# Gate and up products of a mixture of experts in split parts, z heads 4 to 7 moved behind the output products, one activation table for Tanh and Silu

## The chip, the cores and the metric

The kernel runs on one core of a Trainium2 chip, as one launch. The metric is the device time of that launch in microseconds (us), median of several runs. The core has five engines with queues of their own: PE (TensorE, matrix products; PEld is its weight load), DVE (VectorE), ACT (ScalarE), POOL (GpSimd) and SP (SyncE, which issues all DMAs here). They meet only at semaphores.

## The reference

x is 128 tokens of 256 values; ctx is 12544 rows of 256. Three blocks follow one another, each on a layer-normalised x and added to it.

```
x = x + cross_attention(layernorm(x), ctx)            # softmax over 12544 keys
x = x + delta_and_moe(layernorm(x))                   # block 2, below
x = x + ffn(layernorm(x))                             # 8 experts, top 2, W1 256x1024, W2 1024x256

# block 2, input n = layernorm(x)
q, k, v, z = split(rms(n) @ W_qkvz)                   # z: 8 heads of 128
q, k, v = silu(causal_conv4(q, k, v)); g, beta from rms(n) @ W_ba
core = gated_delta_rule(q, k, v, g, beta)             # 8 heads, a recurrence over 128 tokens
core = core * rsqrt(mean(core^2) + eps) * gate_norm * silu(z)
h = n + core @ W_out
y = rms(h)
top two of softmax(y @ W_router), their weights normalised to sum 1 -> route
moe = sum_e route[e] * (silu(y @ W_gate[e]) * (y @ W_up[e])) @ W_down[e]   # 8 experts of 128
out = h + moe
```

The mixture of block 2 takes 256 inputs to 8 experts of 128 (1024 columns) twice, once for gate and once for up.

## The kernel before

All of it stands in one function, `perceiver`, with one block of code per engine; the order of the code is the order of each engine's queue, and `then_inc` / `wait_ge` on named semaphores tie the queues together. There is no scheduler.

Up to about 98 us the cross attention streams ctx in 14 groups. Then come the projections of block 2, and from 119.6 us the delta rule, whose triangular inverse is built in six levels (`for lv in range(1, LEVELS)`). In each level and each half b of the heads PE multiplies pairs (L676), transposes (L457), and multiplies again (L689); DVE masks the first product (`Tm`, L1284) and adds the second to the state (L1300); ACT copies the transposes (`copy_xt`, L967). The state after the add is what the next level's first product waits for. The z heads are projected in between by `project_z(h)`, two products of 128x128x128 each (L462): head 2 in level 2 and heads 3, 5, 7 in the gaps of levels 3, 4, 5 (`Z_GAPS`), heads 4 and 6 at the ends of levels 3 and 4 (`Z_ENDS`).

Behind the levels: Z (L700), the output products o = Z Bv (L707, half b into bank 5 + b), the mean square of o per head (ACT squares L1005, L1008; DVE sums L1315, L1317), its root on ACT (L1012) and reciprocal on DVE (L1323), the product of o and silu(z) (L1319), the scaling of heads by that factor shared by DVE (L1327) and ACT (L1016), `core_transposes` on PE, a scaled copy `coreT` on ACT (L1020) and `project_out` (L718). `keep_warm(n)` (L453) is n products on a constant tile, whose result nobody reads.

Then h (L1334), its transposes, the router product, and `gate_up(b, o, w)`: four times two products that multiply 128 inputs into 512 columns, in plain fp32 (L462). A plain fp32 product shows as two MATMUL records in the trace, a product of fp32r parts as one. Beside it DVE finds the top two experts and their weights (`gates`, L1346 to L1356, then L1361); ACT computes the tangent of the difference (L1029) and Silu of the gate (L1033); DVE multiplies gate, route and up (`prod`, L1368); PE transposes `prod` (`products`), ACT copies it (L1037), and `downs` (L745) multiplies by W_down. Last comes the feed-forward block with 8 large experts, from about 174.5 us, in which weights arrive by DMA into four slots. Slots 2 and 3 lie in `late_slots`, and their first loads wait for the last attention product.

Already in this kernel large products of the attention and of the last block use a split: a matrix a is rounded to fp32r (hi) by a copy, lo = a - hi is rounded too, and three products hi*hi, lo*hi and hi*lo are added in PSUM.

## Time and profile before

| | us |
|---|---|
| median of 3 runs | 232.85 (232.74 to 232.89) |
| the profiled execution's own time | 232.53 |
| its span, first to last instruction | 230.6 |
| PE busy | 221.5 (96%) |
| DVE busy | 143.3 (62%) |
| ACT busy | 143.9 (62%) |
| POOL busy | 122.2 (53%) |

The span leaves out 1.9 us around the first and the last instruction. PE's ends are modelled, so a busy PE need not be limited by its own work. A chain of waits, followed back from the last instruction, tells which work ended last; 74% of it lies on PE. DMA is busy until 121 us (ctx, the weights of block 2, four experts) and again from 178 to 207 us (experts 4 to 7), and idle between.

### The profile page before, as it was taken

Reading aid. Unit: us, or ns where it says so; the run is one execution under the profiler, and the core shown is the slowest. Engines: PE = TensorE matmul, PEld = TensorE weight load, DVE = VectorE, ACT = ScalarE, POOL = GpSimd, SP = SyncE. Lnnn points to the kernel's source line nnn. Section 1 sums busy time; section 2 is a strip of 40 time slices with the busy share of each in tenths; the row PEclk is TensorE's granted clock in tenths of the full one; section 3 lists DMA queues with packets and bytes.
Section 4 is the critical chain, followed back from the end, with each engine's and each line's share of the span. In section 5 each row is a group of like instructions: output and inputs, shape, how many; then the busy total and the mean of one; then the engine's idle time right before and its main releaser. Section 6 shows DMA issues by size and latency. Waiting matters only on the chain.

```text
span 230.6 us, 4195 instructions
## 1 busy us (share of the span) xinstructions
PE 221.5 (96%) x1559; PEld 194.0 (84%) x1559; DVE 143.3 (62%) x339; ACT 143.9 (62%) x264; POOL 122.2 (53%) x80
## 2 busy tenths in 40 slices
PE   8999999999999999889979999989999999999994
PEld 7757878888888888879969999864789999999993
DVE  2346666666666667356995776444334769887783
ACT  5257697777777775348776557545317848677570
POOL 1139878888888897732799910000000544555550
PEclk9999999999999999999999999999999999999999
DMA  6999999999999706999960000000000686960000
GB/s 200 393 430 415 416 420 418 415 418 416 414 419 417 293 3 229 424 423 421 418 283 0 4 0 3 0 0 0 1 3 0 203 345 239 411 259 7 0 0 23
DMA packets 8532, 52.94 MB, mean 230 GB/s; under 512 B 953, under 2 KB 1218, under 8 KB 6466
## 3 DMA queue, kind: packets, MB, share of 16 engines
q1 hardware_dynamic: 8514, 52.69, 56.9%
q8 instruction: 12, 0.20, 0.4%
q14 instruction: 6, 0.05, 0.1%
HBM read 52.56 MB, written 0.13 MB: 228 GB/s over the span
## 4 chain that ended last, share of the span: by engine, by line
PE 74%; DVE 9%; DMA 7%; ACT 4%; POOL 3%; issue 2%; ACTq 0%; DVEq 0%; POOLq 0%
PE psum L462 25%; PE psum L542 11%; PE psum L794 8%; DMA late_sb<-in_ctx_T 7%; PE psum L457 6%; PE psum L518 5%; PE psum L453 3%; PE psum L689 3%; PE psum L676 3%; POOL ctx_lo L375 2%; PE psum L718 2%; PE psum L745 1%; PE psum L560 1%; DVE work L1233 1%; DVE ring L1271 1%
## 5 line engine op out<-in xcount | busy, mean ns | idle before, releaser
L445 POOL TENSOR_TENSOR h_lo<-ring,h_hi 128x512 fp32r<-128x512 f32 x16 | 24.8, 1548 | 67.0 <-ACT h_hi L1061 61.0
L375 POOL TENSOR_TENSOR ctx_lo<-ring,ctx_hi 128x1792 fp32r<-128x1792 f32 x13 | 52.6, 4045 | 14.1 <-ACT ctx_hi L860 14.1
L462 PE MATMUL psum<-late_sb,work 128*128 128x448 f32 x68 | 27.8, 541 | 0.0
L462 PE MATMUL psum<-xT,late_sb 128*128 128x128 f32 x224 | 26.2, 276 | 0.1
L867 ACT ACTIVATE probsT_hi<-psum 128x512 fp32r<-128x512 f32 (+1 forms) x28 | 13.7, 540 | 19.3 <-PE psum L457 18.0
L462 PEld LDWEIGHTS psum<-xT,late_sb 128*128 128x128 f32 x224 | 25.5, 192 | 0.3 <-DVE xT L1377 0.3
L860 ACT ACTIVATE ctx_hi<-ring 128x1792 fp32r<-128x1792 f32 x13 | 22.1, 1701 | 3.4 <-DMA ring<-in_ctx 3.4
L1121 DVE TENSOR_REDUCE smalls<-psum 128x1 f32<-128x896 f32 x14 | 15.3, 1092 | 14.3 <-PE psum L518 9.1
L1145 DVE TENSOR_TENSOR probsT_lo<-psum,probsT_hi 128x512 fp32r<-128x512 f32 (+1 forms) x28 | 16.2, 619 | 7.3 <-ACT probsT_hi L867 7.1
L462 PEld LDWEIGHTS psum<-late_sb,work 128*128 128x128 f32 x68 | 11.9, 190 | 8.1 <-issue 7.8
L457 PE MATMUL psum<-early_sb,work 128*128 128x128 f32 x122 | 17.1, 274 | 0.3 <-ACT work L1016 0.3
L542 PE MATMUL psum<-ctx_hi,probsT_hi 128*128 128x256 f32 x91 | 15.5, 286 | 0.5 <-POOL ctx_lo L375 0.5
L453 PE MATMUL psum<-warm 128*128 128x128 f32 x100 | 14.3, 300 | 1.0 <-POOL smalls L362 1.0
L542 PE MATMUL psum<-ctx_hi,probsT_lo 128*128 128x256 f32 x91 | 15.2, 284 | 0.0
L542 PE MATMUL psum<-ctx_lo,probsT_hi 128*128 128x256 f32 x91 | 15.1, 282 | 0.0
L457 PEld LDWEIGHTS psum<-early_sb,work 128*128 128x128 f32 x122 | 13.9, 143 | 1.3 <-ACT work L850 0.7
L462 PE MATMUL psum<-xT,late_slots 128*128 128x128 f32 x128 | 14.9, 275 | 0.0
L542 PEld LDWEIGHTS psum<-ctx_hi,probsT_hi 128*128 128x128 f32 x91 | 13.5, 189 | 1.4 <-DVE O L1132 0.7
L462 PEld LDWEIGHTS psum<-xT,late_slots 128*128 128x128 f32 x128 | 14.6, 192 | 0.0
L453 PEld LDWEIGHTS psum<-warm 128*128 128x128 f32 x100 | 13.6, 214 | 1.1 <-POOL smalls L362 1.0
L1407 DVE TENSOR_TENSOR w_lo<-late_sb,w_hi 128x1024 fp32r<-128x1024 f32 x8 | 13.6, 1701 | 1.2 <-ACT w_hi L1066 0.8
L850 ACT ACTIVATE work<-psum,smalls 128x896 f32<-128x896 f32 x14 | 14.2, 1011 | 0.1
(262 smaller groups left out, 493.5 us busy)
## 6 DMA issues: line engine op xcount, KB each, us to landing
late_sb<-in_ctx_T SPq DMA_DIRECT2D x14, 896.0 KB, 14.2
ring<-in_ctx SPq DMA_DIRECT2D x14, 896.0 KB, 13.2
late_sb<-in_late SPq DMA_DIRECT2D x10, 825.0 KB, 11.2
late_sb<-in_experts SPq DMA_DIRECT2D x8, 1024.0 KB, 9.9
late_slots<-in_experts SPq DMA_DIRECT2D x8, 1024.0 KB, 11.9
early_sb<-in_early SPq DMA_DIRECT2D x1, 512.0 KB, 3.6
early_sb<-in_early SPq DMA_DIRECT2D x1, 465.0 KB, 17.8
work<-in_levels SPq DMA_DIRECT2D x1, 416.0 KB, 19.1
```

The source lines that it names most:

```text
L375: nc.gpsimd.tensor_tensor(ctxNv[1][:, r % 2], ring[:, r], ctxNv[0][:, r % 2], ALU.subtract).then_inc(s["ctx_lo"], 1)
L445: nc.gpsimd.tensor_tensor(hT[1][:, e % 2, at, :], h32[:, at, :], hT[0][:, e % 2, at, :], ALU.subtract).then_inc(s["h_lo_done"], 1)
L453: nc.tensor.matmul(bank[7][:, 0:P], warm[:, :], warm[:, :], start=True, stop=True)
L457: last = nc.tensor.transpose(o, i, ident)
L462: last = nc.tensor.matmul(o, lhs(c), rhs(c), start=(c == 0), stop=(c == n - 1))
L542: last = nc.tensor.matmul(bank[6 + r % 2][:, 0:D], probsT[a][:, t, :], ctxNv[b][:, r % 2, t, :], start=(i == 0), stop=(i == len(terms) - 1))
L794: last = nc.tensor.matmul(bank[1 + e % 2][:, 0:D], hT[a][:, e % 2, n, :], w2[b][:, e % 2, n, :], start=(t == 0), stop=(t == len(terms) - 1))
L850: nc.scalar.activation(probs[:, :].rearrange("p (z k) -> p z k", z=2), psum[:, 2 * b:2 * b + 2, 0:HALF], ACT.Exp, bias=s_("nb", b, b + 1), ...
L860: nc.scalar.activation(ctxNv[0][:, r % 2], ring[:, r], ACT.Copy).then_inc(s["ctx_hi"], 1)
L867: nc.scalar.activation(probsT[0][:, 4 * q:4 * q + tiles, :], bank[4 + q][:, 0:tiles * P].rearrange("p (t q) -> p t q", q=T), ACT.Copy).the ...
L1121: V.tensor_reduce(s_("mx"), psum[:, 2 * b:2 * b + 2, 0:HALF], mybir.AxisListType.XY, ALU.max).then_inc(s["mx_done"], 1)
L1145: V.tensor_tensor(probsT[1][:, 4 * q:4 * q + tiles, :], bank[4 + q][:, 0:tiles * P].rearrange("p (t q) -> p t q", q=T), probsT[0][:, 4 * q ...
```

## The change

Five edits come together.

1. Gate and up weights are split into hi (ACT, `gate_up_hi(i)`) and lo (POOL, `gate_up_lo(i)`), four pieces of 2 x 512 columns each, in the order of `GATE_UP`; the normalised h, transposed, is split as well (`x2_parts`). `gate_up(i)` on PE is six fp32r products in place of two plain ones. The parts lie where slots 2 and 3 are, so the first loads of these slots now wait for the last of the four `gate_up`.
2. The z heads 4 to 7 leave levels 3, 4 and 5 and follow the output products, ahead of `keep_warm(4)`, which was `keep_warm(10)`. `silu_z(1)` on ACT moves from level 5 to behind the squares of o. In its place in level 5 stands `gate_up_hi(0)`, and `gate_up_hi(1)` stands where the preload of the Sqrt table was.
3. The factor of the mean square is one power of -0.5 on POOL for each half, in place of a root on ACT and a reciprocal on DVE. DVE scales seven heads and ACT one (head 3). The first head's part of `project_out` goes ahead of the second `core_transposes`.
4. Silu's table is loaded ahead of Tanh, by a Silu on a spare value right after the last Sqrt; the separate table load before Silu is gone.
5. `gates` takes fewer dependent steps: route = (e1 + e2) + th (e1 - e2), with the weight already in e1 and e2. The add `xh` moves from ahead of the route to behind it.

The names in the following rows are tiles: `late_sb` holds the weights of block 2, `ring` and `work` are reused buffers, `xT` the transposed input, `warm` the constant tile.

PE, level 4 of the delta rule, from its second half's transposes to the first product of level 5, before:

```order
L457 MATMUL psum<-early_sb,work 128x128 x2
L689 MATMUL psum<-ring 128x128 [waits xt_done,t_done]
L689 MATMUL psum<-ring 128x128
L462 MATMUL psum<-late_sb,xT 128x128 x2
L689 MATMUL psum<-ring 128x128 [waits xt_done,t_done]
L689 MATMUL psum<-ring 128x128
L462 MATMUL psum<-late_sb,xT 128x128 x2
L676 MATMUL psum<-ring,work 128x128 [waits x_done,xc_done,al_high]
```

and now:

```order
L476 MATMUL psum<-early_sb,work 128x128 x2
L708 MATMUL psum<-ring 128x128 [waits xt_done,t_done]
L708 MATMUL psum<-ring 128x128
L708 MATMUL psum<-ring 128x128 [waits xt_done,t_done]
L708 MATMUL psum<-ring 128x128
L695 MATMUL psum<-ring,work 128x128 [waits x_done,xc_done,al_high]
```

Both z heads (L462, two products each) have left this level; nothing stands between its last product and the wait for the state.

PE, from the second half of the output products to `project_out`, before:

```order
L707 MATMUL psum<-ring,work 128x128 [waits zs_done,bv_done,zb_done]
L707 MATMUL psum<-ring,work 128x128 x3
L453 MATMUL psum<-warm 128x128 x10
L457 MATMUL psum<-early_sb,work 128x128 [waits core_act,core_dve]
L457 MATMUL psum<-early_sb,work 128x128 x3
L453 MATMUL psum<-warm 128x128 x4
L457 MATMUL psum<-early_sb,work 128x128 [waits core_act,core_dve]
L457 MATMUL psum<-early_sb,work 128x128 x3
L718 MATMUL psum<-late_sb,ring 128x256 [waits coreT_done]
```

and now:

```order
L724 MATMUL psum<-ring,work 128x128 [waits zs_done,bv_done,zb_done]
L724 MATMUL psum<-ring,work 128x128 x3
L481 MATMUL psum<-late_sb,xT 128x128 x8
L472 MATMUL psum<-warm 128x128 x4
L476 MATMUL psum<-early_sb,work 128x128 [waits core_act,core_dve]
L476 MATMUL psum<-early_sb,work 128x128 x3
L472 MATMUL psum<-warm 128x128 x4
L738 MATMUL psum<-late_sb,ring 128x256 [waits coreT_done]
L476 MATMUL psum<-early_sb,work 128x128 [waits core_dve]
L476 MATMUL psum<-early_sb,work 128x128 x3
```

Eight z products stand where six of the warm ones were, and one product of `project_out` lies between the two sets of transposes.

DVE, from the logits' copy to the first product with the route, before:

```order
L1359 COPY smalls<-psum 128x8 [waits lg_mm,dve_chain]
L1346 MAX smalls<-smalls 128x8 [waits dve_chain]
L1347 MAX_INDEX topi<-smalls 128x8 [waits dve_chain]
L1348 TENSOR_SCALAR smalls<-smalls 128x1 [waits dve_chain]
L1349 CAST smalls<-topi 128x8
L1350 TENSOR_SCALAR smalls<-early_sb,smalls 128x8 [waits dve_chain]
L1351 TENSOR_SCALAR smalls<-early_sb,smalls 128x8 [waits dve_chain]
L1353 TENSOR_SCALAR smalls<-smalls 128x1 [waits tanh_done,dve_chain]
L1354 TENSOR_SCALAR smalls<-smalls 128x1 [waits dve_chain]
L1355 TENSOR_SCALAR smalls<-smalls 128x8 [waits dve_chain]
L1356 SCALAR_TENSOR_TENSOR smalls<-smalls 128x8 [waits dve_chain]
L1361 TENSOR_SCALAR smalls<-smalls 128x8 [waits dve_chain]
```

and now:

```order
L1417 COPY smalls<-psum 128x8 [waits lg_mm,dve_chain]
L1401 MAX smalls<-smalls 128x8 [waits dve_chain]
L1402 MAX_INDEX topi<-smalls 128x8 [waits dve_chain]
L1403 TENSOR_SCALAR smalls<-smalls 128x1 [waits dve_chain]
L1404 CAST smalls<-topi 128x8
L1405 TENSOR_SCALAR smalls<-early_sb,smalls 128x8 [waits dve_chain]
L1406 TENSOR_SCALAR smalls<-early_sb,smalls 128x8
L1409 TENSOR_TENSOR smalls<-smalls 128x8 [waits dve_chain]
L1410 TENSOR_TENSOR smalls<-smalls 128x8
L1414 SCALAR_TENSOR_TENSOR smalls<-smalls 128x8 [waits tanh_done,dve_chain]
L1419 TENSOR_TENSOR xb<-x,hh 128x256 [waits dve_chain]
```

Four of the steps behind the indices are gone and two are new, the wait for the tangent sits at the last one, and the 256-column add (L1419) now lies between the route and its first use.

The core of the diff:

```diff
-Z_GAPS = {2: 2, 3: 3, 4: 5, 5: 7}
-Z_ENDS = {3: 4, 4: 6}
...
-                    sp.wait_ge(s["pv_done"], NG)
+                    sp.wait_ge(s["gu_mm"], 4)
...
+            def gate_up_lo(i):
+                w, b = GATE_UP[i]
+                pool.wait_ge(s["gu_hi"], i + 1)
+                nc.gpsimd.tensor_tensor(gate_up_parts[1][:, w, :, b, :], gate_up_32[:, w, :, b, :], gate_up_parts[0][:, w, :, b, :],
+                                        ALU.subtract).then_inc(s["gu_lo"], 1)
+
+            gate_up_lo(0)
+            for b in range(2):
+                pool.wait_ge(s["ms_done"], b + 1)
+                nc.gpsimd.tensor_tensor(s_("f", 4 * b, 4 * b + 4), s_("ms", 4 * b, 4 * b + 4), s_("marks", 7, 8).to_broadcast([P, 4]), ALU.pow)\
+                    .then_inc(s["f_done"], 1)
+            for i in range(1, 4):
+                gate_up_lo(i)
...
-                if lv in Z_ENDS:
-                    project_z(Z_ENDS[lv])
...
-            keep_warm(10)
+            for h in range(4, HV):
+                project_z(h)
+            keep_warm(4)
             def core_transposes(b):
                 pe.wait_ge(s["core_dve"], b + 1)
-                pe.wait_ge(s["core_act"], b + 1)
+                if b == 0:
+                    pe.wait_ge(s["core_act"], 1)
...
+            project_out(range(0, 1))
             core_transposes(1)
-            project_out(range(0, 4))
+            project_out(range(1, 4))
...
-            def gate_up(b, o, w):
-                wide(bank[o + b][:, :], lambda c: half(xT, c), lambda c: w[:, c, 512 * b:512 * (b + 1)]).then_inc(s["gu_mm"], 1)
+            wide(bank[7][:, 0:E], lambda c: half(xT, c), lambda c: w_router[:, c, :]).then_inc(s["lg_mm"], 1)
+            pe.wait_ge(s["x2_hi"], 2)
+
+            def gate_up(i):
+                w, b = GATE_UP[i]
+                pe.wait_ge(s["gu_hi"], i + 1)
+                terms = [(u, v, c) for u, v in ((0, 0), (0, 1), (1, 0)) for c in range(DC)]
+                for t, (u, v, c) in enumerate(terms):
+                    if t == DC:
+                        pe.wait_ge(s["gu_lo"], i + 1)
+                    if t == 2 * DC:
+                        pe.wait_ge(s["x2_lo"], 2)
+                    last = nc.tensor.matmul(bank[3 + 2 * w + b][:, :], half(x2_parts[u], c), gate_up_parts[v][:, w, c, b, :],
+                                            start=(t == 0), stop=(t == len(terms) - 1))
+                last.then_inc(s["gu_mm"], 1)
...
+            gate_up(0)
+            gate_up(1)
+            gate_up(2)
             products(0)
-            gate_up(1, 5, w_up)
+            gate_up(3)
...
+            def gate_up_hi(i):
+                w, b = GATE_UP[i]
+                if i == 0:
+                    act.wait_ge(s["late2_in"], 16 * (LATE_PARTS - FIRST_PARTS))
+                nc.scalar.activation(gate_up_parts[0][:, w, :, b, :], gate_up_32[:, w, :, b, :], ACT.Copy).then_inc(s["gu_hi"], 1)
...
-            silu_z(1)
+            gate_up_hi(0)
             copy_xt(6)
             keep_columns(6)
-            nc.scalar.activation(s_("spare", 0, 1), s_("eps", 3, 4), ACT.Sqrt).then_inc(s["act_chain"], 1)
-            chain[0] += 1
+            gate_up_hi(1)
...
-                act.wait_ge(s["ms_done"], b + 1)
-                nc.scalar.activation(s_("f", 4 * b, 4 * b + 4), s_("ms", 4 * b, 4 * b + 4), ACT.Sqrt).then_inc(s["f_sd"], 1)
-                act.wait_ge(s["f_done"], b + 1)
-                for k in (2, 3):
-                    h = 4 * b + k
-                    last = nc.scalar.activation(core[:, h, :], core[:, h, :], ACT.Copy, scale=s_("f", h, h + 1))
-                last.then_inc(s["core_act"], 1)
+            silu_z(1)
+            act.wait_ge(s["zo_done"], 1)
+            act.wait_ge(s["f_done"], 1)
+            nc.scalar.activation(core[:, 3, :], core[:, 3, :], ACT.Copy, scale=s_("f", 3, 4)).then_inc(s["core_act"], 1)
             for b in range(2):
                 act.wait_ge(s["core_T"], b + 1)
                 nc.scalar.activation(coreT[:, 4 * b:4 * b + 4, :], bank[3 + b][:, :].rearrange("p (h t) -> p h t", h=4), ACT.Copy,
                                      scale=early_at("gate_norm")).then_inc(s["coreT_done"], 1)
+                if b == 0:
+                    gate_up_hi(2)
+            nc.scalar.activation(s_("spare", 0, 1), s_("eps", 3, 4), ACT.Sqrt).then_inc(s["act_chain"], 1)
+            chain[0] += 1
+            gate_up_hi(3)
...
+            nc.scalar.activation(half(x2_parts[0], 1), bank[2][:, 0:P], ACT.Copy, scale=s_("w2p", 1, 2)).then_inc(s["x2_hi"], 1)
             link(nc.scalar.activation(scratch[:, :], hh[:, :], ACT.Square, accum_out=s_("sd", 0, 1)))
             nc.scalar.activation(s_("sd", 1, 2), s_("sd", 0, 1), ACT.Sqrt, scale=1.0 / D, bias=s_("eps", 2, 3)).then_inc(s["hsd_done"], 1)
+            nc.scalar.activation(s_("spare", 0, 1), s_("eps", 3, 4), ACT.Silu).then_inc(s["act_chain"], 1)
+            chain[0] += 1
...
+            mean_squares(0)
+            gate_output(0)
+            mean_squares(1)
+            normalize(0, range(0, 3))
+            gate_output(1)
+            normalize(1, range(4, HV))
...
+            V.tensor_scalar(half(x2_parts[0], 0), bank[1][:, 0:P], s_("w2p", 0, 1), None, ALU.mult).then_inc(s["x2_hi"], 1)
+            dve.wait_ge(s["x2_hi"], 2)
+            for c in range(DC):
+                V.scalar_tensor_tensor(half(x2_parts[1], c), bank[1 + c][:, 0:P], s_("w2p", c, c + 1), half(x2_parts[0], c),
+                                       ALU.mult, ALU.subtract).then_inc(s["x2_lo"], 1)
...
+                V.tensor_scalar(s_("e1"), early_at("iota"), s_("idf", 0, 1), weight, ALU.is_equal, ALU.mult).then_inc(s["dve_chain"], 1)
+                V.tensor_scalar(s_("e2"), early_at("iota"), s_("idf", 1, 2), weight, ALU.is_equal, ALU.mult).then_inc(s["dve_chain"], 1)
+                chain[0] += 2
+                dve.wait_ge(s["dve_chain"], chain[0])
+                V.tensor_tensor(s_("lg"), s_("e1"), s_("e2"), ALU.subtract).then_inc(s["dve_chain"], 1)
+                V.tensor_tensor(s_("top"), s_("e1"), s_("e2"), ALU.add).then_inc(s["dve_chain"], 1)
+                chain[0] += 2
+                dve.wait_ge(s["dve_chain"], chain[0])
                 dve.wait_ge(s["tanh_done"], turn)
-                link(V.tensor_scalar(s_("w", 0, 1), s_("th"), 0.5, 0.5, ALU.mult, ALU.add))
-                link(V.tensor_scalar(s_("w", 1, 2), s_("th"), -0.5, 0.5, ALU.mult, ALU.add))
-                link(V.tensor_scalar(s_("e1"), s_("e1"), s_("w", 0, 1), None, ALU.mult))
-                return V.scalar_tensor_tensor(out, s_("e2"), s_("w", 1, 2), s_("e1"), ALU.mult, ALU.add)
+                return V.scalar_tensor_tensor(out, s_("lg"), s_("th"), s_("top"), ALU.mult, ALU.add)
...
-            link(V.tensor_copy(s_("lg"), bank[1][:, D:D + E]))
-            link(gates(s_("route"), 1, s_("rs", 0, 1)))
-            link(V.tensor_scalar(s_("route"), s_("route"), s_("rs", 0, 1), None, ALU.mult))
+            link(V.tensor_copy(s_("lg"), bank[7][:, 0:E]))
+            link(gates(s_("route"), 1, s_("rs", 0, 1), s_("w", 0, 1)))
+            link(V.tensor_tensor(xh[:, :], x1[:, :], hh[:, :], ALU.add))
```

## Rows read from the trace of the kernel before

**Rows 1.** The page: granted TensorE clock in 40 slices of the span, in tenths.

```profile
PEclk9999999999999999999999999999999999999999
```

**Rows 2.** Chain of waits, 125 us to the end: start us, us, what.

```profile
132.88 0.45 PE psum L462 x4
...
141.46 1.06 PE psum L707 x8
...
145.91 0.63 PE psum L457 x4
...
148.00 3.59 PE psum L718 x16
...
163.95 2.01 PE psum L745 x8
...
192.80 2.87 PE psum L794 x24
```

**Rows 3.** Timeline, levels 1 and 4 to 6: start us, us, engine line operation, [idle before <-releaser].

```profile
119.64 0.68 PE L676 MATMUL psum<-ring 128*128 128x128 f32 x4 [0.62 <-DVE ring L1271]
...
129.86 0.65 PE L676 MATMUL psum<-work 128*128 128x128 f32 x4
...
131.30 0.68 PE L689 MATMUL psum<-ring 128*128 128x128 f32 x4
...
132.02 0.72 DVE L1300 TENSOR_TENSOR ring<-work,psum 128x256 f32<-128x256 f32 x1
...
133.16 0.61 PE L676 MATMUL psum<-ring,work 128*128 128x128 f32 x4
...
136.41 0.64 PE L676 MATMUL psum<-ring,work 128*128 128x128 f32 x4
...
139.50 1.95 PE L700 MATMUL psum<-ring,work 128*128 128x128 f32 x16
```

**Rows 4.** Timeline and POOL's instructions by form, the output stage.

```profile
143.12 2.31 PEld L453 LDWEIGHTS psum<-warm 128*128 128x128 f32 x20
...
143.99 0.16 DVE L1317 SCALAR_TENSOR_TENSOR smalls<-smalls 128x4 f32<-128x4 f32 x1
...
145.07 0.69 ACT L1016 ACTIVATE work<-work,smalls 128x128 f32<-128x128 f32 x2 [0.40 <-DVE smalls L1323]
145.07 0.48 DVE L1327 TENSOR_SCALAR work<-work,smalls 128x128 f32<-128x128 f32 x2
...
L438 POOL TENSOR_TENSOR smalls<-smalls 128x4 f32<-128x4 f32 x1 | 1.1, 1061 | 0.0
```

**Rows 5.** Timeline, from the router's product to the first product with the route.

```profile
153.13 5.86 PE L462 MATMUL psum<-late_sb,xT 128*128 128x8 f32 x16
...
154.49 0.17 DVE L1359 COPY smalls<-psum 128x8 f32<-128x8 f32 x1
...
155.69 1.28 ACT L1033 ACT_TABLE_LOAD   x1
...
156.99 0.69 ACT L1033 ACTIVATE ring<-psum,smalls 128x512 f32<-128x512 f32 x1
156.99 0.23 DVE L1361 TENSOR_SCALAR smalls<-smalls 128x8 f32<-128x8 f32 x1
...
157.78 1.12 DVE L1368 SCALAR_TENSOR_TENSOR ring<-ring,smalls,psum 128x128 f32<-128x128 f32 x4 [0.55 <-ACT ring L1033]
```

**Rows 6.** Chain of waits, an earlier group: six fp32r products of 448 columns.

```profile
37.55 1.32 PE psum L518 x6
```

**Rows 7.** Instructions by form of 128x1024: the copy to hi, the subtraction.

```profile
L1063 ACT ACTIVATE w_hi<-late_sb 128x1024 fp32r<-128x1024 f32 x4 | 4.2, 1042 | 0.0
...
L399 POOL TENSOR_TENSOR ctx_lo<-ring,ctx_hi 128x1024 fp32r<-128x1024 f32 x1 | 2.4, 2381 | 1.4 <-ACT ctx_hi L896 1.4
```

**Rows 8.** Loads into the slots (line L313), and their first reader in slots 2, 3.

```profile
DMA to landing us min/median/max: 4.9/11.7/21.6
...
181.79 3.40 PE L462 MATMUL psum<-xT,late_slots 128*128 128x128 f32 x29
```

More of the change, by code:

```diff
@@ L99, in perceiver @@
             ctxN = parts(overlay, "ctx", 2 * GT * D)
+        with ExitStack() as overlay:
+            GU = parts(overlay, "gate_up", 2 * DC * E * P)
+        assert 4 * DC * E * P <= (SLOTS - W_SLOTS) * EXPERT_N
         late_slots = sb("late_slots", (SLOTS - W_SLOTS) * EXPERT_N)
@@ L136, in perceiver @@
         w_out = late_at("out", c=HV)
-        w_gate = late_at("gate", c=DC)
-        w_up = late_at("up", c=DC)
         w_down = late_at("down", c=E)
+        gate_up_32 = W_sb[:, LATE["gate"][0]:LATE["up"][1]].rearrange("p (w c b n) -> p w c b n", w=2, c=DC, b=2)
+        gate_up_parts = [part[:, :].rearrange("p (w c b n) -> p w c b n", w=2, c=DC, b=2) for part in GU]
+        x2_parts = [part[:, 0:D] for part in (h_hi, h_lo)]
         w_router = late_at("router", c=DC)
@@ L606, in project_z @@
             def project_z(h):
-                last = wide(bank[5 + h // 4][:, h % 4 * P:(h % 4 + 1) * P], lambda c: half(xT, c),
+                last = wide(bank[5 if h < 4 else 2][:, h % 4 * P:(h % 4 + 1) * P], lambda c: half(xT, c),
                             lambda c: w_qkvz[:, c, CONV + P * h:CONV + P * (h + 1)])
@@ L960, in silu_z @@
                 act.wait_ge(s["z_done"], b + 1)
-                nc.scalar.activation(zs[:, 4 * b:4 * b + 4, :], bank[5 + b][:, :].rearrange("p (h t) -> p h t", h=4), ACT.Silu).then_inc(s["zs_done"], 1)
+                nc.scalar.activation(zs[:, 4 * b:4 * b + 4, :], bank[5 if b == 0 else 2][:, :].rearrange("p (h t) -> p h t", h=4), ACT.Silu).then_inc(s["zs_done"], 1)
             def copy_xt(lv):
@@ L1309, in _, with mean_squares @@
             values(1)
-            dve.wait_ge(s["zs_done"], 2)
             dve.wait_ge(s["n2_read"], 1)
-            for b in range(2):
+            def mean_squares(b):
                 dve.wait_ge(s["osq_done"], b + 1)
@@ L1341, in _, with gates @@
             dve.wait_ge(s["x2_done"], 1)
-            link(V.tensor_tensor(xh[:, :], x1[:, :], hh[:, :], ALU.add))
-            def gates(out, turn, scale):
+            link(V.tensor_scalar(s_("w", 0, 1), s_("rs", 0, 1), 0.5, None, ALU.mult))
+            def gates(out, turn, scale, weight):
                 link(V.max(s_("top"), s_("lg")))
@@ L1385, in _ @@
             link(V.tensor_tensor(s_("lg"), bank[0][:, D:D + E], early_at("rb2"), ALU.add))
-            gates(s_("gate"), 2, 1.0).then_inc(s["gate_done"], 1)
+            gates(s_("gate"), 2, 1.0, 0.5).then_inc(s["gate_done"], 1)
             dve.wait_ge(s["gate_done"], 1)
```

54 lines of the change are left out of this document (24 added, 30 removed).

## The prediction

> **What bounds the kernel now.** I read the page first, then the chain of waits, then the timeline of the three stretches that the change touches. The page has PE busy for 96% of the span (table above), at the full clock of 2.4 GHz in every slice [rows 1]; it does not show whether that is work or warm products. The chain of waits does. In the levels of the delta rule PE's products, the z heads among them, follow one another without a gap, and each z head is a link of 0.45 us [rows 2]. From the output products to the first transposes of `core` (141.46 + 1.06 = 142.52 to 145.91) the chain leaves PE for ACT and DVE, and PE only runs warm products [rows 2, 4]. Then PE again: `project_out`, 3.59 us; the router's and three gate and up products, 5.86 us; `downs` [rows 2, 5]. In the last block PE's 24 products of 2.87 us repeat for each expert [rows 2], and nothing of it is touched except that four loads come later. So three terms decide: A, the levels; B, the stage of the output; C, gate and up with the route.
>
> **A, z heads 4 to 7 out of the levels.** Removed are four heads of 0.45 us [rows 2], 1.8 us of PE in levels 3 (one), 4 (two) and 5 (one). How much of it comes back depends on what is late next. I walk through level 4, from 129.86 to 133.16, 3.30 us [rows 3]. Its second products start after 1.44 us, at 131.30; DVE's add of the first half starts 0.72 us behind that, at 132.02, and takes 0.72 [rows 3]; with a hand-over of 0.05 it releases level 5 at 2.93 us. So 0.4 us of the 0.9 come back, and the rest turns into a wait for DVE. In level 3 the head stood at the end, where the add was already done: its whole 0.45 comes back. Level 5 (133.16 to 136.41, 3.25 us) must hold what level 6 holds on PE, which has no head in it and yet takes from 136.41 to 139.50, 3.09 us, since its second pair of products waits for the copy of the transposes [rows 3]. So 0.15 to 0.25 there. Sum 1.1 us (0.45 + 0.4 + 0.2, rounded up by half a hand-over).
>
> The bounds: 1.8 if all comes back. The other end is that levels 3 and 4 can't go below level 6's 3.1 us either, since DVE has about as much to do in each: 0.15 + 0.2 + 0.15 = 0.5 us come back. I take 1.1, since level 6 has the value products on DVE ahead of its adds, which the others lack.
>
> What hides the new work on ACT: `gate_up_hi(0)`, 1.04 us [rows 7], stands where `silu_z(1)` was, in a pause before `copy_xt(6)`; with everything 0.9 us earlier it ends about when these transposes are ready. If it is late, it is by 0.1 to 0.3 us, inside the bounds. `gate_up_hi(1)`, 1.04, replaces a table load of 1.28 [rows 5]. POOL's `gate_up_lo(0)`, 2.38 us [rows 7], ends some 4 us before POOL's first power is wanted.
>
> **B, the output stage.** Call the end of the first output product 0 (142.52 before). Before, the transposes start at 3.39 and h's operand is ready when `project_out` ends, at 148.00 + 3.59 - 142.52 = 9.07 [rows 2]. Now there are two paths. Power path: the sum of squares is ready at 144.15 - 142.52 = 1.63 [rows 4]; POOL's power of 128x4 took 1.06 us [rows 4], with 0.2 for hand-overs, 2.89; three scalings of 0.24 on DVE [rows 4], 3.6. z path: PE's eight z products start where the warm ones did, at 0.6 [rows 4], and end at 2.4, with drain 2.5; `silu_z(1)` 0.69, 3.2; ACT's one scaling 0.35 [rows 4], 3.55, and 0.15 to PE: 3.7. So the transposes start 0.3 us later than before. Behind them the PE queue is shorter: transposes 0.45, four warm products 0.89, transposes 0.45, eight products of `project_out` 3.59, 5.4 us in place of 5.69 (145.91 to 151.60 [rows 2]), because one of the eight now fills the wait for the second `coreT`. That makes 9.1. `gate_up_hi(2)` lies on ACT ahead of the second `coreT` copy, which then ends at 6.95, 0.45 us before PE wants it. Term B: +0.1 us, between -0.2 (the transposes as early as before) and +0.8 (the second `coreT` late by a further copy of 1.04 us [rows 7], less its 0.45 of slack, and 0.2 on the power). Behind that copy ACT's Sqrt table load (1.28) and `gate_up_hi(3)` (1.04) end near 9.3, while DVE adds h and PE transposes it.
>
> **C, gate, up and route.** Times here are those of before. The plain products start behind the router's at about 153.65: they end at 158.99, and there are 12 records of 512/1.2 ns in it [rows 5]. Six fp32r products of 448 columns took 1.32 us [rows 6], and 24 of 256 columns 2.87 [rows 2]; the first scales to 0.25 us for 512 columns, the second, 0.107 + 0.013, gives 0.226. I take 0.226: 1.36 us for each `gate_up` in place of 1.71. The extra copies `x2_hi` (0.3 us on DVE and on ACT) end with the router's product, and `x2_lo` at 154.05, before PE's fifth product. Three `gate_up` end at 157.7.
>
> Who releases the first `prod`? Before, ACT: table load 155.69 to 156.97, Silu to 157.68, then DVE from 157.78 [rows 5]. Now the table load ends at 155.4 and waits for nothing, and Silu of the gate ends at 156.5. DVE becomes the last: its copy of the logits stays at 154.49, since three small operations replace the add that stood there; from there to the route it took 2.73 us [rows 5], and four steps less with two more and fewer hand-overs make 2.1; then the moved add, 0.45. Products from 157.1 to 158.25, transposes at 158.3 in place of 158.95. So PE waits 0.6 us, and 0.35 of the 0.65 gained are spent there. Behind it the last `gate_up` saves 0.35 and its start delay 0.1. From its end the chain is the same as before (products 1.12, transposes, copy, five `downs`). Term C: -0.65 - 0.45 = -1.1 us. Bounds: -0.5 (0.25 us for each product and 0.4 more on DVE's short steps), -1.6 (the route no bound at all).
>
> The ScalarE: Activation LUTs page of the Trainium skill, section What ACT_TABLE_LOAD costs, says that a switch of tables costs a drain of about 1.38 us besides the 1.28 of the load. The rows of this case speak against it: Silu starts at 156.99, 1.30 us after its load's start [rows 5]. By that page Tanh would come at about 156.8, the route 0.6 us later, and the total at 231.3.
>
> **Loads.** The loads of experts 2 and 3 now start when the last `gate_up` is done, at about 158.0 of the new time. Landing took 21.6 us at the longest, with nine loads ahead or beside, and 11.7 at the median [rows 8]. Their first reader comes at 181.8 - 2.1 = 179.7 [rows 8]. So even the longest, 179.6, is just in time. This costs nothing, and the DMA queue had nothing to do between 121 and 178 us.
>
> **Sum.** -1.1 + 0.1 - 1.1 = -2.1 us against the profiled execution's own 232.53, so 230.4. The median of before is 0.3 us above that execution; the forecast for the median is 230.7.
>
> **Rivals.**
> *Levels bound elsewhere.* DVE and the copies set the pace of the levels, as in level 6 [rows 3]; A is 0.5. For it: level 6 is the only level without a head, and it is hardly shorter. Against it: the walk through level 4, whose add could be done 0.4 us sooner. Time 231.3.
> *The gap moves to the output stage.* Power, z path and the second `coreT` are late; B is +0.8. For it: ACT has four jobs more there, each in a fixed place. Against it: 0.45 us of slack at the narrowest. Time 231.4.
> *PE's clock falls* (slower than before). PE now pauses for 0.85 us before the first transposes of `core` and 0.6 before those of `prod`, where warm products or work ran. If the clock granted falls to 1.2 GHz in the first pause, the 5.4 us behind it take twice as long, +5.4, and nothing hides it: 230.7 + 5.4 = 236.1. It decides as soon as 2.1 us of PE work run at half clock. Against it: before, PE paused for 0.62 us at the start of level 1 and the clock stayed full [rows 1].
> *Experts late.* Landing takes over 22 us; each further us costs one, and 2.1 us of it make the kernel as slow as before. With no other traffic I hold this for the least likely.
> *The table's drain*, above: 231.3.
>
> **How the numbers follow.** Forecast 0.58; levels bound elsewhere 0.15; output stage 0.1; drain 0.03; terms that shrink together until 0.2% or less is left (232.4 to 233.3) 0.06; slower, by the clock 0.05 or late experts and the like 0.03. 0.2%, 0.47 us, is about what a measurement of this kernel can tell from no change. All terms at their good ends give -1.8 - 0.2 - 1.6 = -3.6, 229.2; all at their bad ends -0.5 + 0.8 - 0.5 = -0.2, 232.6. Eight times in ten I expect 229.5 to 232.0. Faster 0.86, same 0.06, slower 0.08.
>
> **What would show it.** A: from the first product of level 4 to the first one behind level 6 9.0 us in place of 9.64, and DVE's add named as what ended PE's wait ahead of level 5. B: from the first output product's end to the end of `project_out` 9.1 us, the transposes at 3.7, released by ACT's scaling. C: from the router's product to the end of `downs` 11.7 us in place of 12.8; the transposes of `prod` wait 0.6 us for DVE; 24 products at 0.226 us. I am wrong if level 4 keeps 3.3 us, if PE's clock shows less than full, or if a large product waits for a load in slot 2.

## The result, and the profile after

| us | before | after |
|---|---|---|
| median | 232.87 (12 runs, 232.46 to 233.88) | 235.68 (12 runs, 233.74 to 238.23) |
| ratio, 95% interval | | 1.0093 [1.007, 1.0117] |
| profiled execution, its span | 232.53, 230.6 | 235.96, 234.2 |

The kernel became 0.9% slower by the ratio; the medians are 2.8 us apart. Forecast was 230.7, with 229.5 to 232.0 as the range. The ratio leaves out one run after, the one of 238.23 us, which counts as slow. The page of the kernel after has PE busy for less of a longer span, and one slice of the granted clock below full, where before had none [rows 1]:

```profile
PE 220.9 (94%) x1555; PEld 195.2 (83%) x1555; DVE 147.1 (63%) x341; ACT 145.2 (62%) x264; POOL 133.5 (57%) x86
...
PEclk9999999999999999999999999979999999999999
```

I cut both spans at the same points of the work. Up to the levels after is 0.32 us late (it is so from 32 us on, behind a load of ctx, and nothing of the change touches that stretch). From the start of level 3 to the first product of Z (L700, now L717) it gains 0.87; from the end of the first output product (L707, now L724, the four heads of half 0) to the end of `project_out` it loses 5.14 (14.22 in place of 9.08); from there to the end of `downs` it gains 1.03; the rest is equal. 0.32 - 0.87 + 5.14 - 1.03 = 3.6, the difference of the spans. So the question is the output stage.

**The levels.** Timeline of after, levels 4 to 6, answering to [rows 3] (start us, us, engine line operation, idle before):

```profile
129.73 0.64 PE L695 MATMUL psum<-work 128*128 128x128 f32 x4
...
131.88 0.62 DVE L1342 TENSOR_TENSOR ring<-work,psum 128x256 f32<-128x256 f32 x1
131.91 0.52 PEld L708 LDWEIGHTS psum<-ring 128*128 128x128 f32 x4 [0.26 <-DVE ring L1326]
...
132.65 0.68 PE L695 MATMUL psum<-ring,work 128*128 128x128 f32 x4
...
134.87 0.52 PEld L708 LDWEIGHTS psum<-ring 128*128 128x128 f32 x4 [0.27 <-DVE ring L1326]
...
135.86 0.64 PE L695 MATMUL psum<-ring,work 128*128 128x128 f32 x4
...
138.96 1.06 PE L717 MATMUL psum<-ring,work 128*128 128x128 f32 x8
```

Level 4 takes 2.92 us in place of 3.30. That is the walk's number (2.93), but not by the walk's wait: DVE's add of the first half (L1342) ended at 132.50, 2.77 us into the level, and in the chain of waits PE's own second pair of products, which had waited 0.26 us for DVE's mask (L1326), ended after it, at 132.62. Level 5 takes 3.21 in place of 3.25: its second pair waits for the mask too. Level 6 keeps 3.10. From the first product of level 4, 9.23 us where the prediction asked for 9.0.

**The output stage.** Timeline of after, 145 to 151 us, answering to [rows 4]:

```profile
145.17 0.39 ACT L1051 ACTIVATE work<-work,smalls 128x128 f32<-128x128 f32 x1
...
145.39 0.68 DVE L1364 TENSOR_TENSOR work<-psum,work 128x512 f32<-128x512 f32 x1
145.63 4.84 POOL L449 TENSOR_TENSOR gate_up_lo<-late_sb,gate_up_hi 128x1024 fp32r<-128x1024 f32 x2
...
145.71 0.63 PE L476 MATMUL psum<-early_sb,work 128*128 128x128 f32 x4 [0.17 <-ACT work L1051]
...
146.10 4.45 DVE L1371 TENSOR_SCALAR work<-work,smalls 128x128 f32<-128x128 f32 x3
...
150.48 0.27 DVE L1374 TENSOR_SCALAR work<-work,smalls 128x128 f32<-128x128 f32 x1
150.81 0.66 PE L476 MATMUL psum<-early_sb,work 128*128 128x128 f32 x4 [3.00 <-DVE work L1374]
```

The first transposes start 3.74 us behind the first output product, where 3.7 was forecast, and ACT's scaling released them. The loss comes behind them. Three scalings of one head on DVE, which wait for nothing, take 4.45 us together. The instructions of that line (count, then minimum, median and maximum in ns, first and last start), those up to 147.9 us of the stretch and all five:

```profile
L1371 DVE TENSOR_SCALAR work<-work,smalls x1: 1977/1977/1977, 146.1 to 146.1; 128x128 f32<-128x128 f32 x1
...
L1371 DVE TENSOR_SCALAR work<-work,smalls x5: 273/286/2360, 144.8 to 148.2; 128x128 f32<-128x128 f32 x5
```

POOL's two subtractions run from 145.63 to 148.00 and from 148.08 to 150.48. The scaling of 146.10 lasts 1.98 us, to 148.08; the next takes 0.27; the third, of 148.2, lasts 2.36, to 150.56. Each long one ends 0.08 us behind a subtraction. DVE's product of the gate, 128x512, which has a source in PSUM, had begun 0.24 us ahead of the first subtraction; neither got longer by the other (0.68 and 2.37 us). PE waits 3.00 us. What follows is slower by itself. Stretches of after: bounds and length; busy time and count of PE, PEld, DVE, ACT, POOL; granted clock, DMA share, GB/s:

```profile
142.00:146.00 4.00, 3.83 (x35) 3.67 (x34) 2.73 (x8) 2.63 (x11) 2.34 (x3) 1.00 0.00 0
146.00:151.00 5.00, 2.00 (x16) 1.53 (x14) 4.72 (x5) 1.63 (x2) 4.39 (x2) 1.00 0.01 3
151.00:156.30 5.30, 5.18 (x18) 3.95 (x17) 0.02 (x1) 3.12 (x4) 1.57 (x1) 0.68 0.00 0
```

Behind the wait the granted clock is 0.68 of the full 2.4 GHz on the mean. In stretches of half a microsecond it is 0.50 (1.2 GHz) from 151.5 to 154.5 us and 1.00 again from 155.0, so it fell when PE had been at work again for some 0.7 us. The 14 products of `project_out` take 4.72 us. The chain of waits of after:

```profile
146.10 4.45 DVE work L1371 x3
...
151.47 4.72 PE psum L738 x14
...
161.66 1.13 DVE ring L1426 x4
...
162.84 0.65 PE psum L476 x4
163.49 1.39 PE psum L767 x6
164.88 1.29 PE psum L778 x6
...
167.51 2.01 PE psum L778 x8
```

**Gate, up and route.** The six fp32r products take 1.39 us, 0.23 each. The transposes of `prod` wait for DVE, at 162.84, by 0.28 us. From the router's product (157.72) to the end of `downs` (169.52) it is 11.80, with 11.7 forecast and 12.83 before [rows 2, 5]. The table, in the timeline of after:

```profile
158.67 1.28 ACT L1067 ACT_TABLE_LOAD   x1
...
159.96 0.20 ACT L1067 ACTIVATE smalls<-smalls 128x1 f32<-128x1 f32 x1
...
160.07 0.19 ACT L1071 ACTIVATE smalls<-smalls 128x1 f32<-128x1 f32 x1
```

**The trace of before already had it.** In its last block DVE's w_lo (128x1024) and POOL's h_lo (128x512) meet, all their tensors in SBUF:

```profile
178.52 1.28 POOL L445 TENSOR_TENSOR h_lo<-ring,h_hi 128x512 fp32r<-128x512 f32 x1 [45.15 <-ACT h_hi L1061]
179.41 1.47 DVE L1407 TENSOR_TENSOR w_lo<-late_sb,w_hi 128x1024 fp32r<-128x1024 f32 x1
180.24 1.77 POOL L445 TENSOR_TENSOR h_lo<-ring,h_hi 128x512 fp32r<-128x512 f32 x1 [0.44 <-ACT h_hi L1065]
181.14 1.95 DVE L1407 TENSOR_TENSOR w_lo<-late_sb,w_hi 128x1024 fp32r<-128x1024 f32 x1 [0.26 <-ACT w_hi L1066]
```

The shortest h_lo takes 1.27 us and the shortest w_lo 1.21. The h_lo of 180.24 began while w_lo ran (to 180.88) and took 0.50 more; the w_lo of 181.14 began while h_lo ran (to 182.01) and took 0.74 more. Whoever comes second is longer, by most of what the first had left.

### The profile page after: what moved, and what is told of

Read it like the earlier page. It is cut to its first block, busy times and chain, and to the rows that moved or that the text cites. A ratio compares the mean times of both kernels' runs of the same rounds, so it can differ in the third digit from the quotient of the medians.

```text
span 234.2 us, 4196 instructions
## 1 busy us (share of the span) xinstructions
PE 220.9 (94%) x1555; PEld 195.2 (83%) x1555; DVE 147.1 (63%) x341; ACT 145.2 (62%) x264; POOL 133.5 (57%) x86
## 4 chain that ended last, share of the span: by engine, by line
PE 72%; DVE 12%; DMA 7%; ACT 4%; issue 2%; POOL 1%; ACTq 0%; DVEq 0%; POOLq 0%
PE psum L481 22%; PE psum L561 12%; PE psum L827 8%; DMA late_sb<-in_ctx_T 7%; PE psum L476 6%; PE psum L537 5%; PE psum L708 3%; PE psum L695 3%; PE psum L472 3%; DVE work L1371 2%; PE psum L738 2%; PE psum L778 1%; PE psum L579 1%; DVE work L1275 1%; DVE ring L1313 1%
## 5 line engine op out<-in xcount | busy, mean ns | idle before, releaser
L1465 DVE TENSOR_TENSOR w_lo<-late_slots,w_hi 128x1024 fp32r<-128x1024 f32 x8 | 13.5, 1686 | 1.2 <-ACT w_hi L1108 1.0
L385 POOL TENSOR_TENSOR ctxT_lo<-late_sb,ctxT_hi 128x512 fp32r<-128x512 f32 x11 | 14.1, 1286 | 0.0
```

The source lines that it names most:

```text
L385: nc.gpsimd.tensor_tensor(Tv[1][:, r % 2, :, 0:POOL_SPLIT], ringT[:, r, :, 0:POOL_SPLIT], Tv[0][:, r % 2, :, 0:POOL_SPLIT], ALU.subtract). ...
L1465: V.tensor_tensor(w2[1][:, e % 2, at], slot_w2(e)[:, at], w2[0][:, e % 2, at], ALU.subtract).then_inc(s["w2_lo_done"], 1)
```

## The experiments

Theory: a DVE instruction of a certain kind stands still while POOL's subtraction runs, for the whole of it; the 1.7 us of clock follow from PE's wait. Rivals: POOL's results are late for some other reason, the scalings are slow by themselves, or the clock is a cost of its own. All edits are to the changed kernel where nothing else is said. Each ratio is against the kernel before on the same chip (median 232.96 us beside experiments 1 to 4, 232.82 beside 5 to 8, 232.76 beside 9 to 12). "Stage" is from the end of the first output product (four heads) to the end of `project_out`.

**1. POOL's order.** `gate_up_lo(1)` ahead of the powers, so that POOL is idle during the scalings.

```diff
             gate_up_lo(0)
+            gate_up_lo(1)
             for b in range(2):
...
-            for i in range(1, 4):
+            for i in range(2, 4):
```

> Only POOL's order changes: the subtraction of the second piece (gate_up_lo(1)) goes ahead of the two powers, into POOL's pause of 4.9 us behind gate_up_lo(0); the third one then can't start before gate_up_hi(2) has ended, at about 148.0, when the second half of core is scaled. Theory (DVE's scaling from SBUF to SBUF is held while a POOL subtraction runs): the four scalings take 1.0 us in place of 4.65, the second set of transposes starts at 147.2 in place of 150.8, PE's clock stays full, project_out takes 3.6 in place of 5.1 us; together about 5.0 us less than the changed kernel, median near 230.8 us. Rival (the scalings wait for something else: their data, or ACT's copy gate_up_hi(2) that runs beside them): they still take over 4 us and the time stays near 235.7.

Measured 230.78 (230.76 to 231.1, 4 runs), ratio 0.989 [0.9846, 0.9935]. Timeline:

```profile
145.82 0.68 DVE L1372 TENSOR_SCALAR work<-work,smalls 128x128 f32<-128x128 f32 x3
...
146.41 0.28 DVE L1375 TENSOR_SCALAR work<-work,smalls 128x128 f32<-128x128 f32 x1
...
147.37 0.60 PE L477 MATMUL psum<-early_sb,work 128*128 128x128 f32 x4
```

The same scalings take 0.87 us, PE waits for none of them, the 14 products take 3.04 us, the stage 9.32. Of the 5.14 us that the stage had lost, 4.90 come back with one subtraction moved; 0.24 are left.

**2. A source in PSUM.** POOL's order as in the changed kernel; product and scaling of the second half become four operations that read o in PSUM.

```diff
-            gate_output(1)
-            normalize(1, range(4, HV))
+            dve.wait_ge(s["zs_done"], 2)
+            dve.wait_ge(s["f_done"], 2)
+            for h in range(4, HV):
+                last = V.scalar_tensor_tensor(core[:, h, :], bank[6][:, (h - 4) * P:(h - 3) * P], s_("f", h, h + 1), zs[:, h, :], ALU.mult, ALU.mult)
+            last.then_inc(s["core_dve"], 1)
```

> POOL's order as in the changed kernel. On DVE, for the second half of the heads the product with silu(z) and the scaling become one operation for each head that reads the output product from PSUM: four operations in place of one of 512 columns and four of 128. POOL's two subtractions run beside them as before. Theory (only the form with all operands in SBUF is held): four operations of 0.34 us each, none long, 1.3 us in all; time about 5 us less than the changed kernel, near 230.7. Rival (any DVE operation is held while POOL subtracts): they take over 4 us again and the time stays near 235.7.

Measured 231.15 (230.63 to 232.31, 10 runs), ratio 0.9931 [0.9903, 0.9959]:

```profile
145.60 4.81 POOL L449 TENSOR_TENSOR gate_up_lo<-late_sb,gate_up_hi 128x1024 fp32r<-128x1024 f32 x2
...
145.75 1.13 DVE L1383 SCALAR_TENSOR_TENSOR work<-psum,smalls,work 128x128 f32<-128x128 f32 x4 [0.31 <-POOL smalls L455]
```

Both engines work at once, neither longer than alone. One of the ten runs (232.31 us) had a mean granted clock of 0.993, though PE's wait is gone in the profiled one.

**3. Small pieces on POOL.** Each subtraction in four of 256 columns.

```diff
-                nc.gpsimd.tensor_tensor(gate_up_parts[1][:, w, :, b, :], gate_up_32[:, w, :, b, :], gate_up_parts[0][:, w, :, b, :],
-                                        ALU.subtract).then_inc(s["gu_lo"], 1)
+                for c in range(DC):
+                    for q in range(2):
+                        at = slice(256 * q, 256 * q + 256)
+                        last = nc.gpsimd.tensor_tensor(gate_up_parts[1][:, w, c, b, at], gate_up_32[:, w, c, b, at], gate_up_parts[0][:, w, c, b, at],
+                                                       ALU.subtract)
+                last.then_inc(s["gu_lo"], 1)
```

> POOL subtracts in pieces of 256 columns, four for each 1024, in the changed kernel's order. Theory as I hold it (a scaling waits until the running POOL instruction ends, then gets its turn ahead of POOL's next): each of the four scalings waits for about one piece of 0.7 us, so the four take some 2.8 us in place of 4.65 and the time falls by 1.8 us, plus what the clock gives back, to 233 or less. Rival (DVE gets its turn only when POOL's queue is empty): the scalings last until the second subtraction ends, as now, or longer, since more instructions mean more start-up; time 235.7 or more.

Measured 232.06 (231.61 to 233.36, 10 runs), ratio 0.9948 [0.9921, 0.9975]:

```profile
145.46 5.53 POOL L452 TENSOR_TENSOR gate_up_lo<-late_sb,gate_up_hi 128x256 fp32r<-128x256 f32 x8
...
145.93 1.72 DVE L1375 TENSOR_SCALAR work<-work,smalls 128x128 f32<-128x128 f32 x3
...
147.57 0.76 DVE L1378 TENSOR_SCALAR work<-work,smalls 128x128 f32<-128x128 f32 x1
```

2.4 us for the four: three of them last 0.76 to 0.77 us, where a piece of POOL's takes 0.73. The engines take turns at the ends of instructions, so the wait scales with POOL's instruction. PE waits 0.75 us.

**4. Warm products in the wait.** DVE held as before, but PE busy.

```diff
             project_out(range(0, 1))
+            keep_warm(14)
             core_transposes(1)
```

> Fourteen warm products (3.1 us of PE) stand in PE's wait for the second half of core, all else is the changed kernel. If the lower clock behind that wait (0.993 over the run, project_out 0.34 us for each record in place of 0.22) comes from PE's idle time, the clock is full again, project_out takes 3.2 us for its last seven heads in place of 4.7, and the median falls by 1.5 us to about 234.1, with less spread from run to run. If the clock has another cause (the state of the chip, the bigger operands), the time stays at 235.7. The scalings stay at 4.65 us either way.

Measured 234.3 (233.62 to 235.56, 10 runs), ratio 1.0049 [1.002, 1.0077]. DVE is held as long as before (4.47 us for three), and the clock stays full:

```profile
145.76 4.47 DVE L1372 TENSOR_SCALAR work<-work,smalls 128x128 f32<-128x128 f32 x3
...
151.00:155.00 4.00, 3.41 (x18) 2.70 (x17) 0.42 (x1) 3.12 (x4) 0.60 (x1) 1.00 0.00 0
```

So the clock is some 1.4 us of the loss by the medians, 1.0 by the ratios (1.0093 against 1.0049), and the wait the rest. The runs of the changed kernel agree in the main: five of its twelve had a mean granted clock of 1.0, and a median of 234.27; seven had 0.985 to 0.993, and 235.91. But two of the five took 235.5 us at full clock, so part of the spread has another source, which was not sought.

**5. Which DVE instructions are held?** I now held the form of one tensor and a scalar for the cause. Test: the same scaling, in the second half, with a second tensor, of ones, in SBUF.

```diff
+                        last = V.scalar_tensor_tensor(core[:, h, :], core[:, h, :], s_("f", h, h + 1), warm[:, :], ALU.mult, ALU.mult)
```

> The changed kernel, POOL's order and all, but the four scalings of the second half are products with a third operand, a tile of ones in SBUF: (core * f) * 1, two tensors read from SBUF, none from PSUM. It settles which form is held. Theory (only the form with one tensor in SBUF and a scalar, which takes 0.28 us for 128 columns where others take 0.34, is held for whole POOL instructions): four operations of 0.35 to 0.5 us each, as DVE's subtractions of the last block are beside POOL's, under 2 us in all, time near 231.5. Rival (every form that lives in SBUF alone is held): over 4 us again, near 235.7.

Measured 235.97 (234.23 to 237.41, 7 runs), ratio 1.0132 [1.0099, 1.0164]:

```profile
145.26 4.79 POOL L449 TENSOR_TENSOR gate_up_lo<-late_sb,gate_up_hi 128x1024 fp32r<-128x1024 f32 x2
...
145.73 4.99 DVE L1374 SCALAR_TENSOR_TENSOR work<-work,smalls,warm 128x128 f32<-128x128 f32 x4
```

My theory fell, the rival held: with all tensors in SBUF this form is held too. Beside experiment 2, what counts is where the sources lie. In the profiled run, 234.23 us, PE waited 3.33 us and its clock stayed full.

**6. Are the levels worth it?** Experiment 1 with the z heads back in the levels (`Z_GAPS`, `Z_ENDS`, `silu_z(1)` and `keep_warm(10)` as before).

> The kernel with POOL's order mended (e1_lo1_early), but z heads 4 to 7 back in levels 3 to 5, silu_z(1) back on ACT in level 5 ahead of gate_up_hi(0), and keep_warm(10) behind the output products. It measures term A by itself. The levels should take 0.9 us more (the changed kernel's level 3 to 6 took 12.27 where before took 13.14), perhaps 0.3 more still if gate_up_hi(0) now delays the transposes' copies of level 6; the output stage 0.1 us less, since the z path is gone and POOL's power path is nearly as long. In all 0.8 to 1.1 us more than e1, near 231.7. Rival (the moved heads gain nothing, they only move the wait): the same time as e1 within 0.3.

Measured 231.65 (231.23 to 232.68, 9 runs), ratio 0.9956 [0.9932, 0.998]. Level 3 to the first product of Z takes 13.14 us against 12.27 in experiment 1, the stage 9.16 against 9.32: by the profiles the move is worth 0.87 - 0.16 = 0.7 us. The median is as expected, but the two medians of the kernel of experiment 1, 230.78 and 231.72 (experiment 11), lie too far apart to confirm it.

**7. Are the split products worth it?** Experiment 1 with plain gate and up products.

> The kernel with POOL's order mended, but gate and up as plain fp32 products on the unsplit tensors, with none of the copies and subtractions of parts. It measures what the split is worth. Three plain gate_up take 5.13 us in place of 4.1, so the transposes of prod start when PE gets to them, 0.4 to 0.5 us later than in e1 (where they wait for DVE), and the last one takes 0.35 more: 0.8 us more than e1; without the copies x2_hi and x2_lo ahead of them DVE's route is 0.3 us sooner, which doesn't help a PE that is busy. Near 231.6. Rival (the split gains the whole PE difference, 4 x 0.35): 1.4 us more. Second rival (the copies cost what the products gain): no difference.

Measured 232.7 (231.42 to 233.34, 10 runs), ratio 0.9981 [0.9956, 1.0005]. Timeline:

```profile
152.93 5.40 PE L757 MATMUL psum<-late_sb,xT 128*128 128x512 f32 x12
...
158.60 1.88 PE L757 MATMUL psum<-late_sb,xT 128*128 128x512 f32 x4
```

From h's transposes to the end of `downs` 13.63 us, against 12.78 in experiment 1: by the profiles the split is worth 0.85 us, as expected. The median is 1.1 us above what was expected; the profiled run took 231.54.

**8. The add later.** Experiment 1 with `xh` behind the first four products with the route.

```diff
-            link(V.tensor_tensor(xh[:, :], x1[:, :], hh[:, :], ALU.add))
...
+                if b == 0:
+                    link(V.tensor_tensor(xh[:, :], x1[:, :], hh[:, :], ALU.add))
```

> The kernel with POOL's order mended, and the add xh (0.43 us on DVE) moved from between the route and its first use to behind the first four products, where DVE waits 2.2 us for PE. In e1 PE waits some 0.6 us for these products. If DVE's route is what holds them (my step C), the transposes start 0.45 us sooner and the kernel takes 0.45 us less than e1, near 230.3. Rival (PE's third gate_up or ACT's Silu would end last next): less than 0.2 us.

Measured 230.61 (230.42 to 230.97, 4 runs), ratio 0.9897 [0.9858, 0.9936]; 12.44 us in place of 12.78, so 0.34 where 0.45 was expected: now PE's third `gate_up` ends last ahead of the transposes of `prod`.

**9. Both at once.** Experiment 8, the four operations of experiment 2, and `silu_z(1)` behind the scaling on ACT.

> Expert 1's product and Silu for the second half moved behind the second core's scaling on ScalarE, and the product with the gate and the scaling of the second half are four operations with one source in PSUM; the POOL order is that of the run with w_lo of expert 1 first, and the add of x hi and x lo stands behind the first four products. Theory (a VectorE operation with a source in PSUM is not held by POOL, and one chain of ScalarE and VectorE ahead of the transposes sets the middle of the output stage): about 0.15 us less than the kernel without this edit (230.6), so 230.4 to 230.5; first transposes 3.6 us behind the first output product, VectorE's four operations 1.1 us together. Rival (the order on ScalarE only moves the wait from the first to the second transposes): 230.6, the output stage 9.3 us as before.

Measured 231.31 (230.07 to 231.93, 6 runs), ratio 0.9931 [0.991, 0.9953]. Chain of waits:

```profile
142.32 1.79 PE psum L482 x16
144.10 0.89 PE psum L473 x8
145.00 0.65 PE psum L477 x4
145.65 0.89 PE psum L473 x8
146.54 0.58 PE psum L739 x2
147.12 0.44 PE psum L477 x4
147.56 3.04 PE psum L739 x14
```

Nothing but PE is left on the chain here; the first transposes start at 3.56 us, the stage takes 9.16, 0.16 less than in experiment 12, as expected. The time missed the expectation: the median is 0.8 us above it, for this kernel's runs spread over 1.9 us, those of 12 over 0.1. Where that spread arises was not tried.

**10. One scaling.** The changed kernel, the four scalings as one operation of 512 columns in SBUF.

```diff
-            normalize(1, range(4, HV))
+            V.tensor_tensor(core[:, 4:8, :], core[:, 4:8, :], s_("f", 4, 8).rearrange("p (h t) -> p h t", t=1).to_broadcast([P, 4, T]),
+                            ALU.mult).then_inc(s["core_dve"], 1)
```

> The changed kernel with the four scalings of the second half as one operation of 512 columns, all three tensors in SBUF; POOL's order unchanged. Theory (VectorE and POOL take SBUF in turns, one instruction each): this one operation waits once, to the end of POOL's first instruction at about 148.0 us, and takes some 0.7 us behind that, so it shows 2 to 3 us instead of the four's 4.7; the second transposes start at about 148.8 in place of 150.8, the output stage takes about 12 us in place of 14.2, and the kernel 233 to 234. Rival (VectorE is held until POOL has done both): the transposes at 151, and 235.7 as the changed kernel. Rival (a broadcast operand makes the operation slow by itself): 149.5 to 150 and 234.5.

Measured 232.03 (231.13 to 232.69, 12 runs), ratio 0.9959 [0.9943, 0.9976]. Timeline, and POOL's four subtractions:

```profile
146.06 2.44 DVE L1383 TENSOR_TENSOR work<-work,smalls 128x512 f32<-128x512 f32 x1
...
148.56 0.66 PE L476 MATMUL psum<-early_sb,work 128*128 128x128 f32 x4 [0.78 <-DVE work L1383]
```

```profile
L449 POOL TENSOR_TENSOR gate_up_lo<-late_sb,gate_up_hi x4: 2352/2365/2670, 136.3 to 152.5; 128x1024 fp32r<-128x1024 f32 x4
```

Held once, to the end of POOL's first instruction (145.60 + 2.36), then 0.5 us of its own; POOL's second is longer by the 0.3 us that it stood behind DVE. The stage takes 10.31 us, not 12, and the time is 1 us under what I expected: PE waits 0.78 us in place of 3.00 and its clock stays full.

**11 and 12. Experiments 1 and 8 again, on one chip.**

> The changed kernel with w_lo of expert 1 ahead of the powers on POOL, once more, for its interval against the kernel before on the chip on which the two other versions run. Theory: 230.8, ratio 0.991 at most, as in the first run. Rival (the first run's chip made it look better): 231.5 or more.

> The version with w_lo of expert 1 first and the add behind the first four products, once more, beside the version without the second edit on one chip. Theory: 0.2 to 0.35 us below it, as the two profiles show (12.44 against 12.78 us from hT to the end of downs). Rival (the gap is given back in the run's median): within 0.1 us of it.

Experiment 1: 231.72 (230.86 to 232.35, 8 runs), ratio 0.9948 [0.9928, 0.9968]. Experiment 8: 230.63 (230.57 to 230.7, 4 runs), ratio 0.99 [0.9877, 0.9922]. The first expectation missed and its rival had the time; whether the chip is the reason is open. The profiled run of 11 comes to ACT's copy of Z at 141.41 us, that of experiment 1 at 140.66, and its span is 0.7 us longer: the same kernel, late ahead of the stage. The second missed on both sides: 1.1 us lie between 11 and 12, more than the add's 0.34. By the profiles the add's move is worth 0.3, and the version of experiment 8 beats both kernels at 230.6, twice.

## Why the prediction was wrong

- **The step that failed** is in term B. Behind the first transposes the prediction counts PE's queue alone, "transposes 0.45, four warm products 0.89, transposes 0.45, eight products of `project_out` 3.59, 5.4 us". So the wait of the second transposes for DVE's scalings of the second half is put at nothing, and no reason is given. The only price of a scaling, "three scalings of 0.24 on DVE", was read where POOL was idle. POOL's subtractions were priced (2.38 us) only as to when the first one ends, not as to what they do to DVE while they run; `gate_up_lo(1)` and `gate_up_lo(2)` were in no term. Measured: the second transposes 3.16 us later than in experiment 1, and B +5.1 in place of +0.1. Experiments 1, 2, 3 and 10 each take the wait away or shorten it by another means, and 5, which keeps all sources in SBUF, does not. Shown.
- **The rival "PE's clock falls"** named 236.1 us, close to the 235.7 measured, by luck (its sign, a clock below full, did come): the loss is 3.2 us of wait and 1.7 of clock, where the rival had 5.4 of clock alone. The clock fell behind that wait, and by less: 1.7 us in the profiled run (4.72 against 3.04), not 5.4. I gave it a pause of 0.85 us as its cause; experiments 3 and 10, with waits of 0.75 and 0.78 us, have the clock full (0.999 or 1.0) in 22 of 22 runs. Behind 3.0 to 3.3 us of waiting it fell in seven of twelve runs of the changed kernel and four of seven of experiment 5 (the waits are those of the profiled runs). Experiment 4, with PE busy in the wait, has it full in ten of ten. So the wait makes the fall likely, not certain, and one run of experiment 2 had a lower clock without such a wait. The rival "the gap moves to the output stage" had the place right and put it at 0.8 us.
- **Term A** was 0.87 for 1.1: level 3 and level 4 gave 0.45 and 0.38 for 0.45 and 0.4, level 5 only 0.04 for 0.2. DVE does set the pace where the heads are gone, but by its mask ahead of the second pair of products; the sign that the prediction asked for, DVE's add as what ends PE's wait ahead of level 5, did not show. That level 4 came out as in the walk is in part luck.
- **Term C** was right: -1.03 for -1.1, 0.23 us for each product for 0.226; the wait for DVE 0.28 for 0.6. DVE's route and add were the last to come, as forecast; moving the add takes 0.34 away (experiment 8).
- **Right besides:** the first transposes at 3.74; loads of experts cost nothing (no large product waits for one); the table costs 1.28 us and no drain, Silu on a spare value starts at 159.96, 1.29 us behind the load's start. The Trainium skill's 1.38 us of drain (ScalarE: Activation LUTs, What ACT_TABLE_LOAD costs) do not show here either.

Without the held scalings the forecast's range would have stood: the same five edits with POOL's order changed (experiment 1) ran at 230.78 and 231.72. Term B was then +0.24 for +0.1.

A rule of the Trainium skill would have told of it: SBUF — State Buffer, section Who interferes with whom, says that VectorE and GpSimd share a port pair as an exclusive lock, that a copy or tensor_scalar with its tensors in SBUF can want it (in a two-port mode), as does an operation with two inputs in SBUF when GpSimd reads SBUF, and that the second to come stands still until the first instruction is done, while an operation outside these modes with at most one input in SBUF is free. The trace agrees in each point that was tried: 2.36 us for a scaling behind a subtraction of 2.39, the same with two inputs in SBUF (experiment 5), none with one input in PSUM (experiment 2). The prediction did not weigh it, nor the four rows of before above.

## What to carry to other kernels

Where work goes to POOL, list what DVE runs in the same stretch and where its tensors lie. An operation with all of them in SBUF takes its turn behind the whole POOL instruction, and several small ones take several turns: put POOL's work ahead, give DVE a source in PSUM, or make one operation of them. A duration read where the neighbour engine is idle is only the lower bound of one where it works. And a wait of 3 us on PE can cost more than itself: in 11 of the 19 runs of the two kernels that had it the granted clock was below full.

## What the runs showed of the hardware

- DVE and POOL take turns instruction by instruction, neither waits until the other's queue is empty; between POOL's two large ones the held DVE instruction and one more got through (1.98 and 0.27 us), and the next was held again (2.36). Four scalings cost 0.87 us alone, 2.4 behind pieces of 0.73 us, 4.65 behind whole subtractions of 2.4; as one operation, 2.44.
- ACT copied 128x1024 in SBUF in 1.05 us from 146.96 beside POOL's subtraction, as long as alone (1.04) [rows 7]: only DVE and POOL were seen to hold each other.
- The power of 128x4 on POOL took 1.01 us, about as before [rows 4]; in the chain of waits of after it is the longest link between the squares and the scaling (1.04 us with its hand-over; DVE's sum has 0.70).
